# In each token step, DVE makes the low part of the weighted x ahead of the addition to the running state, not behind it

## What is computed

```
gate, hBC, dt = split(x @ in_proj_w.T)              # 8192 + 8192 + 2*8*128 + 128 columns
hs, B, C      = split(silu(causal_conv4(hBC)))
dt            = clip(softplus(dt + dt_bias), 0, 100)
xch           = hs * dt                              # x weighted with dt
# for each chunk z of 128 tokens and each head:
Y_diag[z]     = (C B^T * exp(segsum(dt*A))) @ xch    # within the chunk
states[z]     = B^T @ (xch * exp(A_cum[-1] - A_cum)) # what the chunk adds to the state
S[z+1]        = exp(A_cum[-1]) * S[z] + states[z]    # the running state
Y_off[z]      = C @ S[z] * exp(A_cum)
y             = Y_diag + Y_off + hs * D
out           = rmsnorm_by_group(y * silu(gate)) * norm_w @ out_proj_w.T
```

## Time and profile before

| | |
|---|---|
| median of the timed runs | 1803.72 us (1803.08 to 1807.29) |
| the profiled execution: its own time | 1806.34 us |
| its span, first to last instruction | 1804.5 us |
| mean granted TensorE clock | 0.985 of full speed |
| PE busy | 1738.3 us, 96% |
| DVE busy | 1379.1 us, 76% |
| ACT busy | 1078.1 us, 60% |
| POOL busy | 977.6 us, 54% |

### The profile page before, as it was taken

How to read it: one execution, slowest core, us unless ns; L and a number is a source line. 1 busy time by engine, 2 the same in 40 slices (tenths; PEclk the granted TensorE clock), 3 DMA queues, 4 the chain that set the end, 5 groups by cost and what they waited for, 6 DMA issues and landing times.

```text
span 1804.5 us, 31771 instructions
## 1 busy us (share of the span) xinstructions
PE 1738.3 (96%) x9818; PEld 1361.5 (75%) x9818; DVE 1379.1 (76%) x2266; ACT 1078.1 (60%) x1830; POOL 977.6 (54%) x732
## 2 busy tenths in 40 slices
PE   6789999999999999999999999999999999999988
PEld 4567778777777777777787777777777777877776
DVE  4767788777877788777887778777887778876776
ACT  6556665666556666565656665566665656465553
POOL 1436474555546565355646555455754556676651
PEclk9899999999999999999999999999999999999989
DMA  6312121121212122021211212121210212221111
GB/s 229 103 37 70 50 79 45 36 68 56 80 29 74 45 66 63 27 74 56 68 52 36 69 50 79 29 74 51 69 55 26 74 56 74 78 62 60 51 47 59
DMA packets 80936, 112.97 MB, mean 63 GB/s; under 512 B 28402, under 2 KB 32498, under 8 KB 79988
## 3 DMA queue, kind: packets, MB, share of 16 engines
q1 hardware_dynamic: 62898, 78.24, 14.7%
q10 hardware_dynamic: 17858, 32.52, 5.4%
HBM read 88.42 MB, written 22.29 MB: 61 GB/s over the span
## 4 chain that ended last, share of the span: by engine, by line
issue 46%; POOL 36%; PE 10%; ACT 3%; DVE 2%; DMA 1%; SPq 1%; POOLq 1%; ACTq 0%; DVEq 0%
POOL yt L1798 10%; POOL ssq L1793 7%; POOL prev L1775 6%; POOL wg_lo L1700 4%; POOL wo_lo L1700 3%; POOL yt L1801 3%; POOL wx_lo L1700 3%; PE bank L506 2%; PE bank L508 2%; PE bank L507 2%; PE bank L895 1%; PE bank L767 1%; PE bank L902 1%; DMA gate<-w_mod_dram 0%; DMA dtw_d<-xdt 0%
## 5 line engine op out<-in xcount | busy, mean ns | idle before, releaser
L1798 POOL TENSOR_TENSOR yt<-yt,ea 128x384 f32<-128x384 f32 (+1 forms) x128 | 189.7, 1482 | 378.9 <-DVE ea L1608 378.9
L1578 DVE TENSOR_TENSOR lm<-lm,cbm 128x512 f32<-128x512 f32 x256 | 189.4, 780 | 147.7 <-ACT lm L1179 146.9
L1375 DVE SCALAR_TENSOR_TENSOR xc<-bank,bpar,xc 128x511 f32<-128x511 f32 (+2 forms) x384 | 285.3, 743 | 6.8
L506 PE MATMUL bank<-h_hi,wg_hi 128*128 128x512 f32 x640 | 262.0, 409 | 20.3 <-ACT gate L1104 10.4
L508 PE MATMUL bank<-h_hi,wg_lo 128*128 128x512 f32 x640 | 251.1, 392 | 0.0
L507 PE MATMUL bank<-h_lo,wg_hi 128*128 128x512 f32 x640 | 250.4, 391 | 0.0
L1775 POOL TENSOR_TENSOR prev<-prev,dec 128x512 f32<-128x512 f32 x96 | 130.5, 1360 | 154.7 <-DVE prev L1521 92.2
L506 PE MATMUL bank<-h_hi,wx_hi 128*128 128x512 f32 x512 | 211.2, 413 | 2.2 <-DVE bt L1375 2.2
L506 PE MATMUL bank<-wo_hi,g_hi 128*128 128x512 f32 x496 | 206.5, 416 | 0.0
L508 PE MATMUL bank<-h_hi,wx_lo 128*128 128x512 f32 x512 | 201.0, 393 | 0.0
L507 PE MATMUL bank<-h_lo,wx_hi 128*128 128x512 f32 x512 | 200.1, 391 | 0.0
(11 more groups left out here) (222 smaller groups left out, 3943.4 us busy)
## 6 DMA issues: line engine op xcount, KB each, us to landing
raw_w<-w_in_dram SPq DMA_DIRECT2D x145, 256.0 KB, 2.7
raw_w<-w_out_dram SPq DMA_DIRECT2D x64, 256.0 KB, 2.6
part_d<-part ACTq DMA_DIRECT2D x64, 256.0 KB, 2.1
part<-part_d ACTq DMA_DIRECT2D x60, 256.0 KB, 2.7
rt<-rows_d SPq DMA_DIRECT2D x256, 6.0 KB
acc<-x_dram SPq DMA_DIRECT2D x8, 256.0 KB, 6.9
acc<-w_mod_dram SPq DMA_DIRECT2D x2, 1024.0 KB, 6.1
lh<-neg_d SPq DMA_DIRECT2D x128, 6.0 KB
```

Source lines behind the costliest of these rows:

```text
L506: nc.tensor.matmul(out_ap, whi(k), hhi(k), start=(k == 0), stop=False)
L1375: stt(dst[:, at], ps[:, 0:HALF - 3 + k], w(k), dst[:, at], ALU.mult, ALU.add)\
L1578: tt(lm[:, h % 4, :], lm[:, h % 4, :], cbm[:, toks(hf)], ALU.mult).then_inc(v_m, 1)
L1798: tt(yt[:, j % 2, cols], yt[:, j % 2, cols], ea[:, j % 2, cols], ALU.add).then_inc(p_t3, 1)
```

## The change

Within a token step, `new_state(z - 1)` stands in DVE's queue ahead of the instruction that makes `xw_lo`. The change puts it behind. No instruction is added or removed, no wait is changed, and the other engines' queues are the same.

```
                     if z == 3 and not first:
                         accumulate(u, g1, b1, h1, 2, end)
-                    if z >= 1:
-                        new_state(z - 1)
                     if not last and z < NZ - hf:
                         ve.wait_ge(a_xh, sb0 + z + 1)
                         tt(xw_lo[:, z % 2, :], xw[:, z % 2, :], xw_hi[:, z % 2, :].bitcast(F), ALU.subtract).then_inc(x_lo, 1)
+                    if z >= 1:
+                        new_state(z - 1)
                     if not first:
                         if z == 0:
                             group_sums(u, g1, b1, h1)
```

## The result

The changed kernel has a median of 1818.20 us (six runs, 1814.22 to 1819.51), the kernel before, beside it and earlier, 1805.51 us (six runs, 1803.08 to 1807.29). The ratio is 1.0068, with a 95% interval of 1.0058 to 1.0078: slower by 0.68%, 10.5 to 14.1 us. The profiled execution took 1818.01 us, its span is 1816.2 us, 11.7 us more than before. The direction, the places and the mechanism came as forecast; the forecast of 1814.0 us is 4.2 us low, and 1818.2 lies 0.7 us above the range.

The account below looks back on a forecast made before the run. PE was taken to bound the kernel, DVE counting only where PE waits. c = 3 6.65 + c = 0 4.5 - unit 0 0.6 = 10.5 us, on the median 1803.72: 1814 us; range 1804.5 to 1817.5.

Parts of the forecast that it names:

- from the sum to the time: Whole kernel: 10.5 us added to the profiled 1806.34 us gives 1816.9, less 2.6 to the median level, 1814.2, said as 1814.
- What bounds it: Whole kernel: PE is busy 96% of the span, so a change on DVE counts only where PE waits for it.
- c = 1 and 2: Step 1 of these units: xw_lo fills DVE's hole before the state addition, nobody waits for it; cost nothing.
- c = 3, the cover taken away: Third state product: addition behind late xw_hi and xw_lo, acc colliding with POOL's multiply; 0.95 us a unit, 6.65 us in seven.
- The rule on the shared port: DVE against POOL on SBUF: later instruction blocked for the whole other; read strictly, 2.0 us more; forecast kept to the rows.
- c = 0, round by ACT: First Y_diag product: late xw delays ACT's xw_hi, table load, exponentials and first mix; 0.75 us a unit, 4.5 us in six.
- Unit 0: Third state product no longer waits for xw_lo behind the addition; gain 0.6 us, once, bounds 0 and 0.9.
- Does the delay stay: PE's waits at the ends of units, 0.97 us in c = 3: set anew by PE, so no absorption counted.
- The sum: Whole kernel: 6.65 + 4.5 - 0.6 = 10.5 us slower, bounds +5.9 to +12.5.
- One delay alone: Rival: only one of the c = 3 and c = 0 delays, or smaller; +2.5 to +5.9 us, about 1808; chance 0.20.
- Absorbed at the ends of units: Rival: PE's wait of 0.97 us at unit ends absorbs the cost; 0 to +2.5 us, about 1805; chance 0.16.
- faster: Rival: DVE's 0.60 us earliness in c = 1 and 2 reaches PE's waits at unit ends; 1794.7 at most; chance 0.06.

Follow-up runs that it names:

- e1: New order only in unit 0 and in all units c = 1 and c = 2, against the kernel before; ratio 1.0000.
- e10: New order only in step 1 of c = 3, with that step's decay multiply replaced as in e9, against e9; 0.00 us a unit.
- e4: New order only in step 1 of c = 3, against the kernel before; costs 0.54 us a unit.
- e11: New order in all steps of c = 3, with the same multiply replaced as in e9, against e9; 0.58 us a unit, 4.1 us.
- e9: Old order, POOL's decay multiply of step 1 in c = 3 replaced by tiny multiply and memset, against the kernel before; nothing moves, that step's acc 1.07 us.
- e3: New order only in c = 0 of groups 1 to 7, against the kernel before; ratio 1.0036.
- e8: New order with ACT making xw_hi from xdt instead of xw, against the same with the old order; slower by 0.0021, 3.8 us, by the ratios.
- e6: New order with all POOL decay multiplies replaced by tiny multiply and memset, against the same with old order; lost 3.4 us by the units.
- e2: New order only in c = 3, against the kernel before; ratio 1.0045.

## Why the prediction came out as it did

**The step that failed** is the last one, from the sum to the time. I took 1803.72 us, the median of three runs, for the level of the kernel before; six runs gave 1805.51, 1.8 us more. To this come terms of the sum that were too small, by 1.1 us together, c = 3 above all (0.95 put, 1.06 measured). Bound, places and mechanism were right. The parts follow, and the account of the 4.2 us behind them.

**What bounds it, and c = 1 and 2: right.** DVE counted only where PE waits. Shown by e1.

**c = 3, the cover taken away: right, and 0.1 us a unit too small.** Forecast 0.95, measured 1.06, 0.8 us in all. Each step of the working can be set beside the rows after, less 4.85: `xw_lo` of step 1 at 879.72 (put: the same), `acc` 1.50 us long (put: 881.80 to 883.28, which is 1.48), end of `xw` of step 2 at 884.49 (put 884.48), `xw_lo` at 885.19 (885.16), end of the addition at 886.48 (886.43), the product at 886.60 (886.48). So the product is 0.12 us later than put: 0.05 us of it had come together up to the end of the addition, and 0.07 are in the last link, for which I took 0.05 us from the end of DVE's instruction to the start of PE's, by a row where PE waited for `xw_lo`; behind the addition it is 0.12 us. Why it is longer isn't shown; PE's queue has a wait for each of the two. Both halves of the cost are shown apart, the collision by e10 beside e4 and the addition by e11 beside e9. My reading of the old `acc` was incomplete: its 1.07 us already held a wait for POOL's work on weights, and e9, without the multiply, still has 1.07. This changed nothing in the sum.

**The rule on the shared port.** The Trainium skill (SBUF — State Buffer, section Who interferes with whom) would have the blocked instruction wait for the whole of the other. In the profile after, `acc` ends 0.55 us after POOL's multiply (886.65 + 1.50 against 886.54 + 1.06) and takes 0.75 us when it is alone: the direction is the rule's, and e10 shows it with one instruction exchanged, but 0.2 us of the blocked instruction overlap. The rows, to which I kept, gave the right time, and the rule read strictly would have given up to 2.0 us more than they did.

**c = 0, round by ACT: right in place and size.** Forecast 0.75; 0.77 at the first Y_diag product, 0.76 by the unit. Its two parts came too: `acc` of step 1 ends at 945.05 (put: 945.03), and DVE then idles for ACT. e3 shows the place, e8 the wait for ACT, e6 the share of the collision.

**Unit 0: right in kind, 0.6 put and 0.77 read, but too small to be seen.** PE's idle time before the third and fourth state product was 1.18 and 2.13 us. Before, the fourth:

```profile
112.13 0.19 PEld L506 LDWEIGHTS bank<-xw_hi,bt_hi 128*128 128x128 f32 x1 [2.13 <-DVE xw_lo L1562]
```

After, the third and the fourth:

```profile
109.35 0.19 PEld L506 LDWEIGHTS bank<-xw_hi,bt_hi 128*128 128x128 f32 x1 [0.64 <-issue]
...
112.53 0.19 PEld L506 LDWEIGHTS bank<-xw_hi,bt_hi 128*128 128x128 f32 x1 [1.90 <-DVE xw_lo L1560]
```

That is 0.54 + 0.23 = 0.77 us less. The 0.23 us are a collision that is gone: the last `xw_lo` of the unit took 1.58 us beside POOL's multiply before, and takes 0.69 after. e1, which has the same order there, shows 0.65 and 1.90; e2, e3 and e4, with the old order there, show 1.18 and 2.13. But the profiled executions of e1 to e4 come out of unit 0 between 1.6 us before and 2.4 us after the kernel before, whatever their order there.

**Does the delay stay: right.** Once a unit has lost its time, nothing gives it back: over the 14 units of c = 1 and 2 the distance to before grows by 0.4 us in all and doesn't shrink. PE's wait for the convolution at the end of the unit c = 3 (0.97 us) is 1.15 us after.

**The sum and the 4.2 us.** By the parts it is 7.4 + 4.6 + 0.4 - 0.8 = 11.7 us (in hundredths, 7.43 + 4.59 + 0.44 - 0.79), where 0.8 is how much earlier the profile after comes out of unit 0; the spans differ by 11.7. That they agree so well is partly luck, since e1 with the same order in unit 0 comes out of it 2.4 us late. I had 10.55, put as 10.5. Of the 1.1 us that were missing, 0.8 are c = 3, 0.1 c = 0 and 0.4 c = 1 and 2, less 0.2 in unit 0; the 0.4 isn't shown to be the new order's, as e2 has nearly as much (0.35) in these units with the old order.

The rest of the 4.2 us is in the step from the sum to the time. The profiled execution of 1806.34 us with 10.5 us more gives 1816.9, and it came out at 1818.01. I went down from there by 2.6 us to the median of three runs, 1803.72; with three more runs this median is 1805.51, and in later sets of 21 to 30 runs it was 1805.48 to 1807.3. So 1.8 us of the miss come from the level and 0.2 from rounding 1814.2 down. The last 1.0 us lies between the spans, which differ by 11.7, and the medians, which differ by 12.7; the interval of 10.5 to 14.1 us takes in both, and more isn't known of it. The upper end of the range, 1817.5, stood on the low level too: it is 13.8 us above 1803.72, and as far above 1805.51 it would be 1819.3. The ratio of 1.0068 lies just inside the forecast's own +5.9 to +12.5 us (1.0033 to 1.0069).

**The rivals.** One delay alone would be 7.4 (e2) or 4.6 to 5.2 us (after, e3), so both are needed. Absorbed at the ends of units and faster: both fall with e1 and the table by units.

## What to carry to other kernels

Before an instruction that waits is moved ahead of one that doesn't, look at what ends last at that place in each kind of loop step: the one behind may be what hides the wait. Here the same exchange fills a hole in two kinds of units, where nobody needs it, and opens one in the two others, where some 0.5 of 0.6 us of DVE's lateness reach TensorE (0.58 us in e11, 0.52 in e6). When an instruction moves by some tenths of a microsecond, set its new time beside GpSimd's instructions on SBUF: which of the two starts first can be worth as much as the move itself.

## What the runs showed that I had not expected

- How long DVE's blocked instruction takes follows from one number. `acc` and `xw_lo` take 0.75 and 0.69 us free. Every one of them that starts while POOL's decay multiply or its work on weights is under way, 57 in the profile before and 49 in the one after, ends 0.55 us after POOL's instruction, whether it started 0.02 or 1.23 us into it. So `acc` takes 1.07 us when it starts into the last 0.52 us of POOL's instruction, and 1.50 when it starts 0.11 us behind POOL's start.
- Whoever is blocked keeps the wait in its own duration. POOL's decay multiply has a mean of 1360 ns before and 1102 ns after, 130.5 against 105.8 us busy, for the same 96 instructions. DVE didn't take the wait over: all of its `acc` take 66.5 us before and 66.4 after. POOL stands idle instead, 174.9 us ahead of these instructions against 154.7.
- What comes ahead of the loop and behind it varies more from one execution to the next (4 us between e1 and e3 at the end of unit 0) than whole parts of this change cost. Behind the loop it goes with TensorE's granted clock. From 130 us to the last unit the clock is at 2.4 GHz throughout, in every profile; PE is busy there some 98% of the time before and after. In the last 66 to 69 us PE is busy 84 or 85% before and after and 78% in e1, and the clock is at its lower level of 1.2 GHz for a part of them: the mean clock there is 0.84 of full speed before and after, over 69 us, and 0.95 in e1, over 66 us. That before and after are alike there is one reason why their spans compare well. Differences between two profiled executions are better read unit by unit, where unchanged units agree within 0.1 to 0.3 us.
- The releaser that a row names can be the wrong one of two semaphores: at 891.45 it is `xw_lo`, and what was awaited is the addition.
